# One-hots that read their iota from a PSUM bank of VectorE's own, in a two-layer graph network on one Trainium2 core

## Chip, cores and metric

One core of one Trainium2 chip runs the whole kernel as one program. The metric is the device time in microseconds from start to end of one execution. Before the change it is 2472.18 us, the median of three runs (2470.21, 2472.18 and 2474.44).

## The reference

`x` has 6250 rows (nodes) of 256 numbers, and there are 100,000 edges `src -> dst`, sorted by `dst`. Low numbers of `dst` are far more frequent than high ones. What is computed, cut to what matters:

```
xn  = layernorm(x)
agg = segment_sum(xn[src], dst);  cnt = segment_sum(1, dst)
h   = relu(agg / max(cnt,1) @ W1l.T + b1 + xn @ W1r.T)          # layer 1
agg = segment_sum(h[src], dst)
gnn = agg / max(cnt,1) @ W2l.T + b2 + h @ W2r.T                 # layer 2
mix = linear attention over all rows, layer norm, a two-layer MLP with gelu, layer norm
x   = x + gnn + mix
x   = x + ffn(layernorm(x))     # gelu(x@W1+b1), softmax over 8 experts, rows to the best expert's matrix
```

## The kernel before

The rows are cut into 49 tiles of 128, the edges into 197 superchunks of 4 x 128, taken from the highest `dst` to the lowest. For each superchunk GpSimd (POOL) issues four indirect DMAs (L686), which gather 128 rows each from DRAM into one of eight slots of a ring in SBUF. Before it refills a slot, POOL waits at L683 until TensorE has added what lay there. SyncE relays each landed superchunk to TensorE at L596.

VectorE makes the one-hots of a superchunk in one instruction at L856: 4 x 128 columns, `(dst - first row of the tile) == iota`, half precision. Two of its operands are tensors in SBUF (`dst` and `iota16`), and a third, the tile's first row in `tv`, is one number per partition. TensorE multiplies one-hots and gathered rows into the bank `AGG` (L1455), and in layer 1 also one-hots and ones into `CNT` (L1453). A pair of superchunk and tile is an item. There are 245 items in each layer. A table of words tells every engine which items end a tile. The engines take the words apart with register instructions (`Walk`, L447 to L479, whose `kept` is L460, and `Chunks` for TensorE, L481 to L507).

Layer 1 has two stages. In stage A each of 49 turns does the first part of the mixer for one tile and three items. In stage B each of 49 turns does the rest of the mixer for one tile and two items. VectorE's program of a turn of stage B is one list: two statistics, the attention's division (L973 to L978), the sum with the row (L984), nine small steps of a reciprocal root (L422 to L432), the two normalisations (L1007 and L1010), the next two one-hots (L856) and the mixer's residual (L1014). `m_t` in SBUF carries L978 to L984 and L1010 to L1014.

Wherever an item ends a tile, each engine runs its part of `finish1` between its other work. TensorE transposes the hidden rows of two tiles ago (`tr2`, L1461 into the upper half of bank `FT`), makes the product of one tile ago (`out1`, L1480 to L1485 into the lower half of `FO`), the second product of two tiles ago (`r2`, L526 into the lower half of `B7`) and transposes the mean of this tile (`tr1`, into the lower half of `FT`). `r2` waits until VectorE has added the tile before (`residual`, L899). VectorE runs `mean_of` (L883 to L874), `residual` and `hidden` (L892 and L894). ScalarE copies the transposes (L1268 and L1272), applies relu (L1259) and stores the hidden rows for layer 2.

Layer 2 has five items a turn and `finish2` at every tile's end, with much more TensorE work for the expert network. A tail sorts the rows to their experts and runs the expert matrices.

The order within an engine is the written one. Semaphores order the engines: `line.done` counts, `line.wait(e, name, t, n)` waits for that event of tile t - n.

Of the kernel before, what the change touches and what calls it, by code (L numbers as in the profile page):

```python
# [23 lines left out]
P = 128  # L24
N, C, EDGES = 6250, 256, 100000
CH = C // P
TILES = -(-N // P)
LAST_ROWS = N - (TILES - 1) * P
SC = 4
# [138 lines left out]
def build(nc, x, srcL, dstL, dst_tail, w, out):  # L168
    with ExitStack() as ctx:
# [32 lines left out]
        iota16 = sb("iota16", [P, P], F16)  # L202
# [126 lines left out]
        FH = FT[:, C:2 * C]  # L329
        FR = B7  # L330

# [115 lines left out]
        class Walk:  # L447
# [3 lines left out]
            def __init__(self, e, body, n, nu, first):  # L451
                self.e, self.nu, self.u = e, nu, 0
                self.w = e.value_load(words[0:1, n, bass.ds(body, 1)])
                self.k = body * nu + first
                self.t, self.last = self.kept(self.w % 64, TILES - 1), None
                self.c = self.chunk()
# [6 lines left out]
            def chunk(self):  # L463
                return self.kept((self.t + (SUPER - 1 - self.u) - self.k) % 256, SUPER - 1)
# [4 lines left out]
            def ends(self):  # L469

                t = self.t
                self.last = self.kept((self.w >> (6 + self.u)) % 2, 1)
                self.u += 1
                self.t = self.kept(t + self.last, TILES - 1)
                if self.u < self.nu and self.c is not None:
                    self.c = self.chunk()
                return t, self.last
# [8 lines left out]
        class Chunks(Walk):  # L486
# [3 lines left out]
            def __init__(self, e, body, n, nu, first, layer):  # L490
                self.e, self.nu, self.ready, self.items, self.u = e, nu, 1 + layer * SUPER, 1 + layer * ITEMS, 0
                self.w = e.value_load(words[0:1, 3 + n, bass.ds(body, 1)])
                self.k = body * nu + first
                self.set_counts(self.w % 256 + self.ready)
# [4 lines left out]
            def ends(self):  # L499

                k, c, self.u = self.k + self.u, self.c, self.u + 1
                stays = self.kept((self.w >> (7 + self.u)) % 2, 1)
                if self.u < self.nu:
                    self.set_counts(c + stays)
                return lambda: within(self.e, (k + self.ready - c) & 63, TILES - 1), stays
# [213 lines left out]
        def _(e):  # L719
# [13 lines left out]
            step(e.tensor_copy(iota16[:], ii[:, 0:P]))  # L733
            step(e.tensor_copy(iof[:, 0:P + 3], ii[:]))
            step(e.tensor_scalar(ident[:], iof[:, 0:P], iof[:, P + 2:P + 3], None, ALU.is_equal))
            step(e.tensor_scalar(upper[:], iof[:, 0:P], iof[:, P + 2:P + 3], None, ALU.is_gt))
            step(e.memset(ones16[:], 1.0))
# [114 lines left out]
            def one_hot(walk, layer):  # L852

                k, t, c = walk.here()
                e.wait_ge(s_sum, k + (layer * ITEMS + NS + 1 - walk.nu))
                VI.done(e.scalar_tensor_tensor(  # L856
                    S[:, walk.u, :, :], dst[:, bass.ds(c * SC, SC)].unsqueeze(2).to_broadcast([P, SC, P]),
                    tv[:, bass.ds(k, 1)], iota16[:].unsqueeze(1).to_broadcast([P, SC, P]),
                    ALU.subtract, ALU.is_equal), "S")
# [19 lines left out]
            def finish1(t, g, mix_done):  # L879
# [20 lines left out]
                if isinstance(t, int):  # L900
                    part(e, t, 0, mean_of)
                    part(e, t, 3, residual)
                    part(e, t, 2, hidden)
                else:
                    t = Turn(e, t, (0, 1))
                    mean_of(t)
                    with e.If(t.base > 2):
                        residual(t - 3)
                        hidden(t - 2)
                    with e.If(t.base == 2):  # L910
                        hidden(t - 2)
# [48 lines left out]
            def to_stats(i, first, second, items):  # L960
# [10 lines left out]
                if first:  # L971
# [7 lines left out]
                    m_t.rearrange("p (h q m) -> p h q m", h=CH, m=HD), blocks[:, :, 0:P].rearrange("p h (q m) -> p h q m", m=HD),  # L979
# [4 lines left out]
                step("s", at(lambda: e.scalar_tensor_tensor(m_s[:], xnS, rstd[:, bass.ds(raw(i), 1)], m_t[:], ALU.mult, ALU.add)))  # L984
# [14 lines left out]
            def from_stats(i, first, second, meanwhile=lambda: None):  # L999
# [10 lines left out]
                step("n2", mo(lambda: e.scalar_tensor_tensor(m_t[:], m_o, lnt[:, 2:3], lng2, ALU.subtract, ALU.mult)))  # L1010
# [3 lines left out]
                step("res", mo(lambda: e.scalar_tensor_tensor(res_tile(i - 2), m_t[:], lnt[:, 7:8], res_tile(i - 2),  # L1014
# [24 lines left out]
            def finish2(t, g):  # L1039
# [5 lines left out]
                def x2(t):  # L1045
                    PO2.wait(e, "o", t)
                    VX2.done(e.tensor_tensor(res_tile(t), res_tile(t), FO[:, 0:C], ALU.add), "x2")
# [160 lines left out]
        def _(e):  # L1208
# [46 lines left out]
            def finish1(t):  # L1255
                def relu(t):
                    PH1.wait(e, "h", t)
                    VB1.wait(e, "hlo", t, 1)
                    AR1.done(e.activation(hb[:], FO[:, 0:C], ACT.Relu), "relu")  # L1259
# [164 lines left out]
        def _(e):  # L1424
# [39 lines left out]
            def finish1(t):  # L1464
# [3 lines left out]
                def tr2(t):  # L1468
# [4 lines left out]
                    PB1.done(transposes(FT, C, hb), "tr2")  # L1473

                def out1(t):
# [3 lines left out]
                    for h in range(CH):  # L1479
                        e.matmul(FO[:, 0:C], xTs[:, h, :], w1r[:, h, :], start=(h == 0), stop=False)  # L1480
                    e.matmul(FO[:, 0:C], ones3[:], gb1, start=False, stop=False)
                    if isinstance(t, int):
                        AM1.wait(e, "mT", t)
                    for h in range(CH):
                        ins = e.matmul(FO[:, 0:C], mT[:, h, :], w1l[:, h, :], start=False, stop=(h == CH - 1))  # L1485
                    PH1.done(ins, "h")

                def r2(t):
                    AH1.wait(e, "hT", t)
                    VR1.wait(e, "res", t, 1)  # L1490
# [3 lines left out]
                def tr1(t):  # L1494
                    VM1.wait(e, "mean", t)
                    clear(AGG[:])
                    clear(CNT[:, 0:1])
                    PT1.done(transposes(FT, 0, mean), "tr1")
# [86 lines left out]
            def finish2(t):  # L1585
                def out2(t):
                    AM2.wait(e, "mT", t)
                    PO2.done(matmuls(e, FO[:, 0:C], [(mT[:, h, :], w2l[:, h, :]) for h in range(CH)]), "o")
# [30 lines left out]
                def tr1(t):  # L1619
                    VM2.wait(e, "mean", t)  # L1620
                    clear(AGG[:])
                    PT2.done(transposes(FT, 0, mean), "tr1")
# [114 lines left out]
```

## Time and profile before

| | us |
|---|---|
| median of the three runs | 2472.18 |
| lowest and highest run | 2470.21, 2474.44 |
| span of the profiled execution | 2464.9 |
| median less that span | 7.3 |
| busy: TensorE (PE), GpSimd (POOL), VectorE (DVE), ScalarE (ACT) | 1925.4, 1692.3, 1145.2, 561.3 |
| mean granted clock of TensorE, of full speed | 0.888 |

The profiled execution's own time is not listed apart from its span. The span goes from the first to the last instruction, and what lies around it is taken as the 7.3 us to the median. The profile has views of one execution: how busy each engine is, which instruction waited for which, the chain of work that ended last, groups of instructions by line, and the instructions in order of time. "Issue" is time in which an engine waited for nothing that the profile shows. A letter q behind an engine (DVEq) marks its sequencer, which runs waits and register instructions. Times in the views are counted from the start of the span.

### The profile page before, as it was taken

What the parts mean: (1) busy time and instruction counts of PE and PEld (TensorE: products, weight loads), DVE (VectorE), ACT (ScalarE), POOL (GpSimd) and SP (SyncE); (2) the same over time, 40 slices, a digit from 0 to 9 for tenths busy, and PEclk for the clock granted to TensorE, in tenths of its full rate; (3) what the DMA queues carried; (4) which work ended last, traced back from release to release, by engine and by line L of the source; (5) the groups of instructions that cost most, each with busy time, mean ns of one, the idle gap of its engine ahead of it and who ended that gap; (6) DMA issues with size and microseconds to landing.
All of it is one profiled execution on the core that took longest, in us unless ns stands there. A gap on an engine that the chain in (4) does not pass through costs nothing.

```text
span 2464.9 us, 41722 instructions
## 1 busy us (share of the span) xinstructions
PE 1925.4 (78%) x9589; PEld 1194.8 (48%) x9590; DVE 1145.2 (46%) x3187; ACT 561.3 (23%) x1270; POOL 1692.3 (69%) x1759
## 2 busy tenths in 40 slices
PE   2599988888688877786899999877764543679998
PEld 1255555555355555553455555443332211368886
DVE  6444444434377777775655555443322221252221
ACT  5544433333122222221222222111110000101110
POOL 4577777777777777775777777777777777264442
PEclk9999999989799999987999999887876665789999
DMA  5444444444444444443455545454444333235551
GB/s 175 136 125 121 126 124 121 120 119 122 121 137 132 131 134 134 134 128 106 154 174 158 172 148 174 137 164 125 151 126 132 115 115 105 97 138 167 166 167 64
DMA packets 155421, 332.58 MB, mean 135 GB/s; under 512 B 35285, under 2 KB 89527, under 8 KB 155349
## 3 DMA queue, kind: packets, MB, share of 16 engines
q0 software_dynamic: 85824, 248.21, 34.4%
q10 hardware_dynamic: 42630, 58.35, 6.8%
q1 hardware_dynamic: 26898, 25.33, 3.3%
q14 instruction: 54, 0.44, 0.1%
q8 instruction: 15, 0.25, 0.0%
HBM read 273.97 MB, written 58.72 MB: 135 GB/s over the span
## 4 chain that ended last, share of the span: by engine, by line
POOL 34%; PE 28%; issue 16%; DVE 11%; DMA 3%; DVEq 3%; POOLq 2%; ACT 2%; SPq 0%; ACTq 0%
POOL big L686 34%; PE bank L526 8%; PE bank L1687 8%; PE bank L1455 4%; PE bank L1675 2%; DVE S L856 1%; DMA mbuf<-qT_d 1%; PE bank L1461 1%; DVE m_s L984 1%; POOLq L683 1%; PE bank L1610 1%; DVE m_t L978 1%; POOL big L696 1%; DVE res L1014 1%; PE bank L1485 1%
## 5 line engine op out<-in xcount | busy, mean ns | idle before, releaser
L686 POOL DMA_INDIRECT big<-xh_d,edges x782 | 772.9, 988 | 243.6 <-issue 231.3
L686 POOL DMA_INDIRECT big<-hh_d,edges x782 | 750.1, 959 | 256.9 <-issue 231.5
L1455 PE MATMUL bank<-big,S 128*128 x1960 | 591.1, 427 | 249.0 <-SPq L596 237.1
L856 DVE SCALAR_TENSOR_TENSOR S<-edges,tv,iota 128x512 f16<-128x512 f16 x490 | 365.2, 753 | 430.0 <-PE bank L1455 289.9
L1455 PEld LDWEIGHTS bank<-big,S 128*128 128x128 f16 x1960 | 204.1, 104 | 535.8 <-issue 393.0
L1453 PE MATMUL bank<-ones,S 128*128 128x1 f16 x980 | 166.8, 170 | 72.3 <-SPq L596 55.4
L526 PE MATMUL bank<-turned,x1T 128*128 128x512 f32 x392 | 194.4, 618 | 0.0
L707 POOL DMA_INDIRECT out_dram<-big,node_s x56 | 56.8, 1014 | 145.1 <-DVE big L1189 139.0
L1383 ACT ACTIVATE x1T<-bank 128x256 f32<-128x256 f32 x49 | 18.9, 385 | 527.9 <-PE bank L1461 527.8
L1453 PEld LDWEIGHTS bank<-ones,S 128*128 128x128 f16 x980 | 96.0, 98 | 86.9 <-SPq L596 67.3
L1189 DVE SCALAR_TENSOR_TENSOR big<-bank,prob_s,res 128x256 f32<-128x256 f32 x56 | 27.1, 484 | 179.3 <-PE bank L1689 179.3
L526 PEld LDWEIGHTS bank<-turned,abuf 128*128 128x128 f32 x784 | 96.2, 194 | 24.0 <-issue 23.0
L1397 ACT ACTIVATE mbuf<-bank 128x512 f32<-128x512 f32 x98 | 58.5, 597 | 201.9 <-PE bank L526 201.9
L1687 PE MATMUL bank<-big,abuf 128*128 x448 | 101.9, 381 | 0.0
L1687 PE MATMUL bank<-big,mbuf 128*128 x448 | 101.4, 379 | 0.0
L526 PEld LDWEIGHTS bank<-turned,x1T 128*128 128x128 f32 x392 | 66.4, 189 | 69.5 <-issue 69.5
L526 PE MATMUL bank<-turned,mbuf 128*128 128x512 f32 x196 | 97.0, 619 | 0.0
L872 DVE TENSOR_SCALAR lo<-bank,RC 128x256 f32<-128x256 f32 x98 | 47.4, 484 | 103.6 <-PE bank L1455 82.0
L526 PE MATMUL bank<-turned,abuf 128*128 128x8 f32 x784 | 91.7, 252 | 0.8 <-ACT abuf L1389 0.8
L1552 PE MATMUL bank<-mbuf 128*128 128x132 f32 x196 | 35.9, 307 | 68.6 <-DMA mbuf<-qT_d 68.6
L1687 PEld LDWEIGHTS bank<-big,abuf 128*128 128x128 f32 x448 | 83.5, 191 | 10.3
L1687 PEld LDWEIGHTS bank<-big,mbuf 128*128 128x128 f32 x448 | 82.9, 190 | 10.2
(228 smaller groups left out, 2927.0 us busy)
## 6 DMA issues: line engine op xcount, KB each, us to landing
hx_d<-mbuf ACTq DMA_DIRECT2D x49, 512.0 KB
big<-xh_d,edges POOLq DMA_INDIRECT x782
big<-hh_d,edges POOLq DMA_INDIRECT x782
big<-in_fwd_dram SPq DMA_DIRECT2D x8, 1024.0 KB, 6.1
xh_d<-big SPq DMA_DIRECT2D x49, 128.0 KB, 2.2
qT_d<-abuf ACTq DMA_DIRECT2D x49, 128.0 KB
hh_d<-HL ACTq DMA_DIRECT2D x49, 128.0 KB
mbuf<-qT_d ACTq DMA_DIRECT2D x49, 128.0 KB
```

The source lines that it names most:

```text
L526: ins = eng.matmul(out_ap, a, b, start=(n == 0), stop=(n == len(pairs) - 1))
L686: e.indirect_dma_start(G[:, r, n % SC, :], None, table, bass.IndirectOffsetOnAxis(ap=srcx[:, n:n + 1], axis=0)).then_inc(d_g[r], 16)
L707: e.indirect_dma_start(out, bass.IndirectOffsetOnAxis(ap=node_s[:, i:i + 1], axis=0), o_sb[:, u, :], None, bounds_check=N - 1, oob_is_err= ...
L856: VI.done(e.scalar_tensor_tensor(S[:, walk.u, :, :], dst[:, bass.ds(c * SC, SC)].unsqueeze(2).to_broadcast([P, SC, P]), tv[:, bass.ds(k, 1 ...
L872: line.done(e.tensor_scalar(lo[:], AGG[:, C:2 * C], rc, None, ALU.mult), "lo")
L1189: VO.done(e.scalar_tensor_tensor(o_sb[:, u % OB_SLOTS, :], (B6, FT)[u % 2][:, 0:C], prob_s[:, bass.ds(i, 1)], RB[:, u, HID:HROW], ALU.mult ...
L1397: AG2.done(e.activation(Hb[:, b * 512:b * 512 + 512], pb[4 + b][:], ACT.Gelu), f"g{b}")
L1453: e.matmul(CNT[:, 0:1], S[:, walk.u, j, :], ones16[:, 0:1], start=False, stop=False, skip_group_check=True)
L1455: ins = e.matmul(AGG[:], S[:, walk.u, j, :], G[:, bass.ds(slot, 1), j, :].rearrange("p a c -> p (a c)"), start=False, stop=False, skip_gro ...
L1552: ins = e.matmul(B4[:, h * (P + 4):(h + 1) * (P + 4)], qS[:, h, :], KVs[:, h, :], start=True, stop=True)
L1675: ins = e.transpose(((B4, B5), (FO, B7))[u % 2][b][:, q * P:(q + 1) * P], RB[:, u, (b * 4 + q) * P:(b * 4 + q + 1) * P], ident[:])
L1687: e.matmul(acc, (HT, HT2)[u % 2][:, j, :], wd[:, bass.ds(ex, 1), j, :].rearrange("p a c -> p (a c)"), start=(j == 0), stop=False)
```

## The change

The constant 0 to 127 moves from `iota16` (SBUF, half precision) to `numbers_p`, the lower half of bank `FO` (PSUM, full precision), and L856 reads it there. The mixer's temporary `m_t` of stage B moves to `m_p`, the upper half of `FO`. Only VectorE uses this bank then, until the tail. To free it, the product of `out1` and `out2` goes to the upper half of `FT` (`FU`), and the transposes of `tr2` go to the upper half of `B7` (`FH`). TensorE's waits follow the banks: `tr2` now waits for `residual` of the tile before (it was `r2`), `tr1` in layer 1 waits for relu of the tile before, and `tr1` in layer 2 for `x2` of the tile before. VectorE's `finish1` does `residual` before `mean_of`. All remainders by a power of two in the walks become bit masks.

```diff
-        iota16 = sb("iota16", [P, P], F16)
...
-        FH = FT[:, C:2 * C]
+        FH = B7[:, C:2 * C]
         FR = B7
+        FU = FT[:, C:2 * C]
+        numbers_p, m_p = FO[:, 0:P], FO[:, C:2 * C]
...
-                self.t, self.last = self.kept(self.w % 64, TILES - 1), None
+                self.t, self.last = self.kept(self.w & 63, TILES - 1), None
...
-                return self.kept((self.t + (SUPER - 1 - self.u) - self.k) % 256, SUPER - 1)
+                return self.kept((self.t + (SUPER - 1 - self.u) - self.k) & 255, SUPER - 1)
...
-                self.last = self.kept((self.w >> (6 + self.u)) % 2, 1)
+                self.last = self.kept((self.w >> (6 + self.u)) & 1, 1)
...
-                self.set_counts(self.w % 256 + self.ready)
+                self.set_counts((self.w & 255) + self.ready)
...
-                stays = self.kept((self.w >> (7 + self.u)) % 2, 1)
+                stays = self.kept((self.w >> (7 + self.u)) & 1, 1)
...
-            step(e.tensor_copy(iota16[:], ii[:, 0:P]))
...
+            step(e.tensor_copy(numbers_p, iof[:, 0:P]))
...
-                    tv[:, bass.ds(k, 1)], iota16[:].unsqueeze(1).to_broadcast([P, SC, P]),
+                    tv[:, bass.ds(k, 1)], numbers_p.unsqueeze(1).to_broadcast([P, SC, P]),
...
                     t = Turn(e, t, (0, 1))
-                    mean_of(t)
                     with e.If(t.base > 2):
                         residual(t - 3)
-                        hidden(t - 2)
-                    with e.If(t.base == 2):
+                    mean_of(t)
+                    with e.If(t.base > 1):
                         hidden(t - 2)
...
-                    m_t.rearrange("p (h q m) -> p h q m", h=CH, m=HD), ...
+                    m_p.rearrange("p (h q m) -> p h q m", h=CH, m=HD), ...
...
-  step("s", ... m_s[:], xnS, rstd[:, bass.ds(raw(i), 1)], m_t[:], ...)
+  step("s", ... m_s[:], xnS, rstd[:, bass.ds(raw(i), 1)], m_p, ...)
...
-  step("n2", ... m_t[:], m_o, lnt[:, 2:3], lng2, ...)
+  step("n2", ... m_p, m_o, lnt[:, 2:3], lng2, ...)
...
-  step("res", ... res_tile(i - 2), m_t[:], lnt[:, 7:8], res_tile(i - 2), ...)
+  step("res", ... res_tile(i - 2), m_p, lnt[:, 7:8], res_tile(i - 2), ...)
...
-                    VX2.done(e.tensor_tensor(res_tile(t), res_tile(t), FO[:, 0:C], ALU.add), "x2")
+                    VX2.done(e.tensor_tensor(res_tile(t), res_tile(t), FU, ALU.add), "x2")
...
-                    AR1.done(e.activation(hb[:], FO[:, 0:C], ACT.Relu), "relu")
+                    AR1.done(e.activation(hb[:], FU, ACT.Relu), "relu")
...
-                    PB1.done(transposes(FT, C, hb), "tr2")
+                    VR1.wait(e, "res", t, 1)
+                    PB1.done(transposes(B7, C, hb), "tr2")
...
                 def r2(t):
                     AH1.wait(e, "hT", t)
-                    VR1.wait(e, "res", t, 1)
...
+                    AR1.wait(e, "relu", t, 1)
                     PT1.done(transposes(FT, 0, mean), "tr1")
...
-                    PO2.done(matmuls(e, FO[:, 0:C], [...]), "o")
+                    PO2.done(matmuls(e, FU, [...]), "o")
...
+                    VX2.wait(e, "x2", t, 1)
                     PT2.done(transposes(FT, 0, mean), "tr1")
```

In `out1` the four matmuls and the bias write `FU` in place of `FO[:, 0:C]` as well.

## Rows read from the trace of the kernel before

**Rows 1.** Timeline (start us, us) of POOL: its one wait for a slot over 0.3 us.
```profile
1377.19 1.45 POOL L686 DMA_INDIRECT big<-hh_d,edges  x1 [1.00 <-PE bank L1455]
```

**Rows 2.** Line L686: ns min/median/max, first and last start.
```profile
L686 POOL DMA_INDIRECT big<-xh_d,edges x782: 942/946/1440, 95.1 to 1104.9; - x196
```

**Rows 3.** Gathers by stretch (A, B, layer 2 to 1500, after): busy us, mean ns.
```profile
L686 POOL DMA_INDIRECT big<-xh_d,edges x428 | 424.7, 992 | 135.7 <-issue 128.3 <-DMA xh_d<-big 5.6 <-PE bank L1455 1.8
...
L686 POOL DMA_INDIRECT big<-xh_d,edges x354 | 348.2, 983 | 107.9 <-issue 103.0 <-PE bank L1455 4.9
...
L686 POOL DMA_INDIRECT big<-hh_d,edges x295 | 285.2, 967 | 108.5 <-issue 84.7 <-DMA hh_d<-HL 18.3 <-PE bank L1455 5.6
...
L686 POOL DMA_INDIRECT big<-hh_d,edges x487 | 464.9, 955 | 148.3 <-issue 146.8 <-PE bank L1455 1.5
```

**Rows 4.** Waits of PE: 300 to 650 us, then 1125 to 2113 us.
```profile
PE bank L1453 <- SPq L596: 46.4, 17, 3.8
...
PE bank L1455 <- SPq L596: 233.9, 80, 13.9
```

**Rows 5.** Timeline (start us, us): first and last gather held by a one-hot.
```profile
116.65 1.44 DVE L856 SCALAR_TENSOR_TENSOR S<-edges,tv,iota 128x512 f16<-128x512 f16 x2 [1.50 <-issue]
...
117.03 1.19 POOL L686 DMA_INDIRECT big<-xh_d,edges  x1 [0.30 <-issue]
...
1988.22 0.96 POOL L686 DMA_INDIRECT big<-hh_d,edges  x1 [0.30 <-issue]
```

**Rows 6.** Timeline: first and last gather that starts inside a PSUM-reading DVE operation.
```profile
114.14 0.48 DVE L872 TENSOR_SCALAR lo<-bank,RC 128x256 f32<-128x256 f32 x1
114.53 0.95 POOL L686 DMA_INDIRECT big<-xh_d,edges  x1 [0.31 <-issue]
...
1976.99 0.95 POOL L686 DMA_INDIRECT big<-hh_d,edges  x1 [0.30 <-issue]
```

**Rows 7.** Chain that ended last, one turn of stage B: shares, then start us, us.
```profile
by line: issue 21.2%; DVE S L856 6.5%; DVE m_s L984 5.8%; DVE res L1014 5.6%; DVEq L460 5.4%; DVE m_t L978 5.1%; DVE lnt L986 5.1%; DVEq L1028 5.1%; DVE lnt L965 4.0%; DVEq L453 3.5%; DVEq L856 3.0%; DVE lnt L423 2.9%; DVE lnt L431 2.8%; DV
...
856.41 0.31 DVEq L460
...
857.02 0.33 DVE S L856
```

**Rows 8.** Waits of DVE, 720 to 1105 us; then the next turn's one-hots in the timeline.
```profile
DVE S L856 <- issue: 7.7, 30, 0.3
...
865.66 1.55 DVE L856 SCALAR_TENSOR_TENSOR S<-edges,tv,iota 128x512 f16<-128x512 f16 x2 [0.27 <-issue]
```

**Rows 9.** Register instructions of PE's sequencer: ns min/median/max.
```profile
L497 PEldq FUSED_REGOPS  x147: 126/180/188, 97.3 to 2091.8; - x147
...
L1521 PEldq FUSED_REGOPS  x147: 82/90/135, 111.1 to 2116.1; - x147
```

**Rows 10.** DVE operations of 256 columns by form: busy us, mean ns.
```profile
L872 DVE TENSOR_SCALAR lo<-bank,RC 128x256 f32<-128x256 f32 x98 | 47.4, 484 | 103.6 <-PE bank L1455 82.0 <-issue 19.8
L874 DVE SCALAR_TENSOR_TENSOR mean<-bank,RC,lo 128x256 f32<-128x256 f32 x98 | 47.4, 484 | 3.5
...
L984 DVE SCALAR_TENSOR_TENSOR m_s<-mbuf,rstd,m_t 128x256 f32<-128x256 f32 x49 | 23.7, 484 | 11.6 <-DVE m_t L978 11.2 <-issue 0.2
...
L1051 DVE TENSOR_SCALAR m_t<-res,lnt 128x256 f32 x48 | 21.8, 453 | 1.8
...
L894 DVE TENSOR_TENSOR HL<-hb,HL 128x256 f16<-128x256 f32 x49 | 21.1, 431 | 1.7
...
L899 DVE TENSOR_TENSOR res<-res,bank 128x256 f32 x46 | 19.0, 412 | 0.0
```

**Rows 11.** Timeline, a stage-B turn that ends a tile.
```profile
889.35 1.10 PE L526 MATMUL bank<-w2r,hT 128*128 128x256 f32 x4 [1.35 <-DVE res L899]
...
894.88 0.39 ACT L1342 ACTIVATE mbuf<-bank 128x256 f32<-128x256 f32 x1 [2.07 <-PE bank L1574]
...
895.85 0.42 DVE L965 BATCH_NORM_STATS2 lnt<-mbuf 128x6 f32<-128x256 f32 x1
```

More of the change, by code:

```diff
@@ L900, in finish1 @@
                 if isinstance(t, int):
+                    part(e, t, 3, residual)
                     part(e, t, 0, mean_of)
-                    part(e, t, 3, residual)
                     part(e, t, 2, hidden)
@@ L978, in to_stats @@
                 step("tz", at(lambda: e.tensor_tensor(
-                    m_t.rearrange("p (h q m) -> p h q m", h=CH, m=HD), blocks[:, :, 0:P].rearrange("p h (q m) -> p h q m", m=HD),
+                    m_p.rearrange("p (h q m) -> p h q m", h=CH, m=HD), blocks[:, :, 0:P].rearrange("p h (q m) -> p h q m", m=HD),
                     zd.rearrange("p (h q) -> p h q", h=CH).unsqueeze(3).to_broadcast([P, CH, P // HD, HD]), ALU.mult)))
@@ L983, in to_stats @@
                     e.wait_ge(d_lx, raw(i) * 16 + 16)
-                step("s", at(lambda: e.scalar_tensor_tensor(m_s[:], xnS, rstd[:, bass.ds(raw(i), 1)], m_t[:], ALU.mult, ALU.add)))
+                step("s", at(lambda: e.scalar_tensor_tensor(m_s[:], xnS, rstd[:, bass.ds(raw(i), 1)], m_p, ALU.mult, ALU.add)))
                 after("s")
@@ L1009, in from_stats @@
                     after("n1")
-                step("n2", mo(lambda: e.scalar_tensor_tensor(m_t[:], m_o, lnt[:, 2:3], lng2, ALU.subtract, ALU.mult)))
+                step("n2", mo(lambda: e.scalar_tensor_tensor(m_p, m_o, lnt[:, 2:3], lng2, ALU.subtract, ALU.mult)))
                 got = meanwhile()
                 after("n2")
-                step("res", mo(lambda: e.scalar_tensor_tensor(res_tile(i - 2), m_t[:], lnt[:, 7:8], res_tile(i - 2),
+                step("res", mo(lambda: e.scalar_tensor_tensor(res_tile(i - 2), m_p, lnt[:, 7:8], res_tile(i - 2),
                                                               ALU.mult, ALU.add)))
@@ L1479, in out1 @@
                     for h in range(CH):
-                        e.matmul(FO[:, 0:C], xTs[:, h, :], w1r[:, h, :], start=(h == 0), stop=False)
-                    e.matmul(FO[:, 0:C], ones3[:], gb1, start=False, stop=False)
+                        e.matmul(FU, xTs[:, h, :], w1r[:, h, :], start=(h == 0), stop=False)
+                    e.matmul(FU, ones3[:], gb1, start=False, stop=False)
                     if isinstance(t, int):
@@ L1484, in out1 @@
                     for h in range(CH):
-                        ins = e.matmul(FO[:, 0:C], mT[:, h, :], w1l[:, h, :], start=False, stop=(h == CH - 1))
+                        ins = e.matmul(FU, mT[:, h, :], w1l[:, h, :], start=False, stop=(h == CH - 1))
                     PH1.done(ins, "h")
@@ L1587, in out2 @@
                     AM2.wait(e, "mT", t)
-                    PO2.done(matmuls(e, FO[:, 0:C], [(mT[:, h, :], w2l[:, h, :]) for h in range(CH)]), "o")
+                    PO2.done(matmuls(e, FU, [(mT[:, h, :], w2l[:, h, :]) for h in range(CH)]), "o")
                 def trx(t):
```

## The prediction

> **What bounds the kernel now.** I read the waits of POOL first, then the gathers by line and stretch, then PE's waits, then the chain of waits inside one turn of stage B. POOL hardly ever waits for a free slot of the ring. In layer 1 what stands before the gathers of stage B is 107.9 us for 354 of them, 0.305 us each and nearly all "issue" [rows 3]. In layer 2 it idles longer for a slot only once, 1.00 us at 1377 us [rows 1]. So both layers run at POOL's pace of 0.946 us [rows 2] plus 0.305 us a gather, and what a gather takes beyond 0.946 us is the only slack in it. That excess is 428 x 46 ns = 19.7 us in stage A, 354 x 37 ns = 13.1 us in stage B, 295 x 21 ns = 6.2 us in layer 2 up to 1500 us and 487 x 9 ns = 4.4 us after it [rows 3], some 43 us in all.
>
> The timeline shows what it is. A gather that starts while a one-hot runs lasts until shortly after the one-hot's end: at 116.65 us two one-hots run back to back (1.44 us), and the gather of 117.03 us takes 1.19 us [rows 5]. From the first to the last [rows 5] I count 131 such gathers with together 31.9 us of excess: 67 with 15.8 us in stage A, 30 with 7.8 us in stage B, 34 with 8.4 us in layer 2 (5.5 us of it after 1377 us). In stage B 18 more lie behind L984, with 1.0 us. Behind VectorE operations that read PSUM it isn't so. 125 gathers start inside L872, L874, L899, L978 or L1047, and all but one take 0.95 us or less, as the first and the last [rows 6]. (The one takes 1.05 us, and an operation with two SBUF tensors follows there.) So a one-hot with its iota in PSUM should hold no gather up.
>
> POOL isn't the only limit. In stage A TensorE waits for landed data, 46.4 us of the 350 us from 300 on [rows 4], so that POOL sets the end of stage A. In stage B the chain of a turn holds VectorE and its sequencer alone [rows 7]: it is VectorE's list that takes the time, 8.6 us a turn (its one-hots start at 857.02 us [rows 7] and at 865.66 us [rows 8]), while POOL runs ahead and is caught up only at the end. In layer 2 TensorE is close to full until about 1460 us, as the one wait for a slot shows [rows 1], and after it waits for data (233.9 us over the layer) [rows 4].
>
> **The change, part by part.**
>
> *One-hots off the gathers.* 31.9 us of excess go, where POOL's pace is what counts: 15.8 us in stage A in full. In stage B POOL gains 7.8 + 1.0 us (L984 now reads one tensor from SBUF, L1010 still reads two). In layer 2 the 2.9 us before 1377 us are lost to TensorE, and 5.5 us after it are kept. The gathers slide against the other operations, so each term may be off by a fifth.
>
> *Masks for remainders.* In stage B they are on the path. Before the first one-hot of a turn the sequencer loads a word and runs L460 with two remainders, 0.31 us [rows 7], and VectorE idles for it, 7.7 us in 30 times, 0.26 us each [rows 8]. What a remainder costs: on TensorE's sequencer L497 (one remainder, one sum) takes 180 ns, and L1521 (a sum, a difference, one mask) 90 ns [rows 9]. With one simple step less on the dearer side I take 0.12 to 0.13 us for each. Two of them are the 0.26 us. The two one-hots of a turn take 1.55 us together [rows 8], with the sequencer's remainders between them, where two back to back take 1.44 us [rows 5], so 0.11 us more go. That is 0.37 us a turn, 17.4 us over 47 full turns. If a mask costs as much as a remainder it is nothing. On POOL nothing changes, on ScalarE and TensorE the sequencers run ahead, and I count nothing.
>
> *PSUM in VectorE's own list.* Six operations of a turn read or write `FO` now (two L856, L978, L984, L1010, L1014). L874 reads one PSUM tensor and L984 none, and both take 484 ns [rows 10]; that is the same kind of instruction as the one-hot, so I take nothing. The ends: 484 less 453 ns (L872 against L1051) is 31 ns more, 412 less 431 ns (L899 against L894) 19 ns less [rows 10], so over 6 x 47 operations +8.7 or -5.4 us. Writes to PSUM by VectorE have no row, and I give them the same ends. The Trainium skill speaks against the change here (VectorE: DVE Perf Modes, the errata section): it gives a fixed 120 cycles to an operation from PSUM and 58 to one from SBUF, 65 ns more. The rows of L874 and L984 don't show it. By that rule four reads a turn would cost 12 us.
>
> *The moved wait on TensorE.* In stage B VectorE reaches `finish1` after L986. In 6 of the 11 tile ends from 687 us on, TensorE is there first, and `r2` already stands 1.35 us or less for L899 [rows 11]. Now `tr2` stands, and behind it `out1` (2.1 us, which ran meanwhile before). With `residual` first, VectorE releases it at 887.8 us, and in the same order as before TensorE is done about 1.15 us later. Behind it are the MLP's products, ScalarE's L1342 and VectorE's L965. L1342 ended at 895.27 and L965 started at 895.85 [rows 11], which would now be 895.5. So some 0.9 us a time are exposed, 5.4 us in all. In stage A the same wait costs TensorE about 0.4 us at about half of the ends, hidden by the ring, whose slots are free over 20 us before POOL needs them. `tr1` waits for relu behind `r2` (1.3 us against 0.38 us), and in layer 2 for `x2` behind 7 us of expert products: nothing. If these covers went, each would cost the length of the wait itself, under 0.5 us at 49 ends.
>
> *Setup, tail, queues.* The constant is one VectorE copy as before, no DMA is added or moved, and POOL and SyncE get no new wait: nothing.
>
> **The sum.** Stage B's list ends 15.8 + 17.4 - 5.4 = 27.8 us earlier, POOL's last gather of layer 1 15.8 + 8.8 = 24.6 us, with about 1 us of margin behind it. The later of the two decides: 25 us. Layer 2 adds 5.5 us. Together 30.5 us from a span of 2464.9 us, 2434.4 us. The median lies 7.3 us above this span, so I forecast 2441.7 us.
>
> **The rivals.**
> 1. *Masks are no cheaper than remainders.* For it: the register instructions on VectorE differ in length for other reasons too (L460 covers several steps). Against it: rows 9. Stage B gains nothing of its own, and the exposed waits shrink to about 3 us: 15.8 - 3 + 5.5 = 18 us, 2454 us. Chance 0.12.
> 2. *PSUM costs more in the list,* by the size that the skill's page gives (65 ns) on four reads a turn, 12 us: 27.8 - 12 + 5.5 = 21 us, 2451 us. The same mechanism at 31 ns on six is 8.7 us and 2448 us. Against it: 484 and 484 ns. Chance 0.13.
> 3. *The gathers are not released,* because `dst` and the scalar `tv` are still read from SBUF. Then POOL keeps its pace, VectorE's faster list only waits for data, and the gain is the 1 us of margin: 2471 us. Against it: L874 too reads a tensor and a scalar from SBUF, and no gather waits behind it. Chance 0.04.
> 4. *Slower: stage B's list itself.* Place: the six PSUM operations a turn, above all the writes of L978 and L1010, which nothing in the trace shows, and what waits on them. All other gains together are 27.8 + 5.5 = 33 us, so it decides from 33 / 282 = 118 ns an operation on. At 150 ns it is 42 us of cost, 9 us slower, 2481 us. Against it: every PSUM reader in the trace. Chance 0.04.
>
> **How the numbers follow.** The forecast has 0.67. Its own bounds are the fifth on the gathers' terms (5 us), the PSUM ends (-5 to +9 us, the gain capped by POOL's pace) and the exposed waits (0 to 5 us): 2432 to 2450 us. To hold 8 in 10 it reaches to the middle of rivals 1 and 2, to 2458 us, and on the fast side to 2431 us. Under 0.2% (5 us) a measurement of this kernel can't tell from no change. Faster by more: 0.67 + 0.12 + 0.13 = 0.92. Rival 3 is within: 0.04. Rival 4: 0.04.
>
> **What would show it.** Right: mean gathers near 0.95 us in all stretches, and those inside one-hots at 0.95 us; L460 at 0.1 to 0.2 us; turns of stage B near 8.25 us without a tile's end; one-hots still at 0.75 us; a wait of L1461 on L899 of about 2 us at 6 ends. Wrong: gathers inside one-hots still long (rival 3), L460 at 0.3 us (rival 1), one-hots or L978, L984, L1010, L1014 longer by 50 ns or later behind each other (rivals 2, 4), or many more waits of POOL for a slot, which would say that another engine took over the bound.

## Result, and the profile after

The changed kernel takes 2488.61 us, the median of four runs (2485.78 to 2497.58), against 2471.95 us for the kernel before beside it. The ratio is 1.0076, 95% interval 1.0054 to 1.0097: 0.76% slower, where the prediction said 2441.7 us and gave slower a chance of 0.04. In the new code every line below 900 lies two further down, later ones mostly one (L686 is L688, L856 is L858, L899 is L901). The page of the changed kernel:

```profile
span 2484.0 us, 45558 instructions
...
PE 1928.5 (78%) x9589; PEld 1185.4 (48%) x9590; DVE 1144.4 (46%) x3187; ACT 560.4 (23%) x1270; POOL 1655.8 (67%) x1759
...
q14 instruction: 275, 2.25, 0.3%
```

POOL is busy 36.5 us less than before (1692.3), VectorE and TensorE are busy as long as before to within 3.1 us, and the span has grown by 19.1 us. It isn't TensorE's clock, whose granted share is 0.896 after and 0.888 before. Two counts don't fit a change of banks: the instructions went from 41722 to 45558, and the DMA queue that brings code (packets, MB, share) has 275 packets, where the page of before has:

```profile
q14 instruction: 54, 0.44, 0.1%
```

The groups of the changed kernel by line answer to [rows 3] and [rows 10]:

```profile
L688 POOL DMA_INDIRECT big<-xh_d,edges x782 | 744.3, 952 | 267.0 <-issue 229.6 <-PE bank L1456 31.7 <-DMA xh_d<-big 5.6
L688 POOL DMA_INDIRECT big<-hh_d,edges x782 | 742.1, 949 | 287.1 <-issue 228.1 <-PE bank L1456 31.5 <-DMA hh_d<-HL 27.5
...
L858 DVE SCALAR_TENSOR_TENSOR S<-edges,tv,bank 128x512 f16<-128x512 f32 x490 | 365.5, 747 | 571.0 <-issue 298.1 <-PE bank L1456 268.5 <-DVE mbuf L1008 1.9
...
L1011 DVE SCALAR_TENSOR_TENSOR bank<-mbuf,lnt,turned 128x256 f32<-128x256 f32 x49 | 23.8, 485 | 0.3 <-DVEq L126 0.3
L985 DVE SCALAR_TENSOR_TENSOR m_s<-mbuf,rstd,bank 128x256 f32<-128x256 f32 x49 | 23.5, 481 | 11.3 <-DVE bank L979 11.2
...
L979 DVE TENSOR_TENSOR bank<-bank,mbuf 128x256 f32<-128x256 f32 x49 | 21.2, 433 | 1.7
```

The gathers are released: 952 and 949 ns on average, where the stretches of layer 1 had 992 and 983. Of those that start while a one-hot runs, 318 now, none takes over 0.96 us and the mean is 945 ns; before it was 230 with a mean of 1085 ns. The one-hot takes 747 ns (753 before). What is new stands in the idle time: POOL waits 63 us for slots of the ring, and the one-hots stand 298 us on "issue".

Where the 19 us are, I read from first and last starts. Stage B goes from the first to the last start of the sum with the row, layer 2 from the first to the last gather of `hh_d`. For the changed kernel (ns min/median/max, first to last start):

```profile
L985 DVE SCALAR_TENSOR_TENSOR m_s<-mbuf,rstd,bank x49: 479/481/482, 654.6 to 1113.0; 128x256 f32<-128x256 f32 x49
```
```profile
L688 POOL DMA_INDIRECT big<-hh_d,edges x782: 940/946/1719, 1128.1 to 2128.8; - x196
```

and for the kernel before:

```profile
L984 DVE SCALAR_TENSOR_TENSOR m_s<-mbuf,rstd,m_t x49: 483/484/486, 672.5 to 1109.4; 128x256 f32<-128x256 f32 x49
```
```profile
L686 POOL DMA_INDIRECT big<-hh_d,edges x782: 942/946/1717, 1124.3 to 2112.0; - x196
```

Stage B now begins 17.9 us earlier, takes 458.4 us instead of 436.9 (21.5 more), layer 2 takes 1000.7 instead of 987.7 (13.0 more), and what follows the last gather 355.2 instead of 352.9. So stage A brought what was hoped for, and stage B and layer 2 each lost something of their own. The same rows of every later kernel give the table further down.

In stage B, it is mostly the tile ends: the nine turns with one took 11.1 to 12.8 us before and take 11.1 to 15.2 us now, 16.7 us more in all. The 39 others are 0.12 us longer each, 4.8 us in all. The waits from 654 to 1113 us (us in total, times, longest):

```profile
PE bank L1462 <- DVE res L901: 21.4, 9, 3.3
```

This is the moved wait. The timeline of one such turn (start us, us) shows what stands behind it:

```profile
928.71 0.43 DVE L987 BATCH_NORM_STATS2 lnt<-m_s 128x6 f32<-128x256 f32 x1
929.37 0.42 DVE L901 TENSOR_TENSOR res<-res,bank 128x256 f32 x1 [0.23 <-issue]
...
929.93 0.66 PE L1462 MATMUL bank<-ident,hb 128*128 128x128 f32 x2 [3.27 <-DVE res L901]
...
930.39 1.91 PE L1482 MATMUL bank<-w,xTs 128*128 128x256 f32 x4
...
932.55 1.45 PE L1487 MATMUL bank<-w,mT 128*128 128x256 f32 x4
...
933.84 1.03 PE L528 MATMUL bank<-w2r,hT 128*128 128x256 f32 x4
...
935.51 1.06 PE L528 MATMUL bank<-x1T,turned 128*128 128x128 f32 x8
...
937.79 0.75 DVE L858 SCALAR_TENSOR_TENSOR S<-edges,tv,bank 128x512 f16<-128x512 f32 x1 [1.32 <-PE bank L1456]
```

TensorE idles 3.27 us, then does `out1` (until 934 us), which before ran while `r2` was not yet due, then `r2`, the new mean's transpose and the mixer's products, and only then the item whose sum VectorE's second one-hot waits for.

For layer 2 the waits of VectorE from 1205 to 2113 us, after and before:

```profile
DVE S L858 <- issue: 224.6, 150, 7.9
DVE S L858 <- PE bank L1456: 188.8, 75, 7.9
```
```profile
DVE S L856 <- PE bank L1455: 233.2, 99, 5.2
...
DVE S L856 <- issue: 69.1, 124, 1.8
```

The one-hots wait 155 us longer for nothing that the profile names, up to 7.9 us at once, while 239 of the 275 code packets arrive in this stretch (19 before). Much of this takes the place of other waits, such as the one-hots' own on TensorE (44 us less); layer 2 as a whole is 13.0 us longer.

### The profile page after: what moved, and what is told of

Read it like the earlier page. It is cut to its first block, busy times and chain, and to the rows that moved or that the text cites. A ratio compares the mean times of both kernels' runs of the same rounds, so it can differ in the third digit from the quotient of the medians.

```text
span 2484.0 us, 45558 instructions
## 1 busy us (share of the span) xinstructions
PE 1928.5 (78%) x9589; PEld 1185.4 (48%) x9590; DVE 1144.4 (46%) x3187; ACT 560.4 (23%) x1270; POOL 1655.8 (67%) x1759
## 3 DMA queue, kind: packets, MB, share of 16 engines
q14 instruction: 275, 2.25, 0.3%
## 4 chain that ended last, share of the span: by engine, by line
PE 36%; POOL 20%; issue 17%; DVE 13%; DVEq 6%; DMA 3%; ACT 3%; POOLq 1%; ACTq 1%; SPq 0%
POOL big L688 19%; PE bank L528 11%; PE bank L1690 8%; PE bank L1456 6%; PE bank L1678 2%; DVEq L462 2%; PE bank L1462 2%; PE bank L1487 2%; PE bank L1482 1%; DMA mbuf<-qT_d 1%; DVE m_s L985 1%; PE bank L1612 1%; DVE bank L979 1%; DVEq L455 1%; DVEq L858 1%
## 5 line engine op out<-in xcount | busy, mean ns | idle before, releaser
L688 POOL DMA_INDIRECT big<-hh_d,edges x782 | 742.1, 949 | 287.1 <-issue 228.1
L688 POOL DMA_INDIRECT big<-xh_d,edges x782 | 744.3, 952 | 267.0 <-issue 229.6
L858 DVE SCALAR_TENSOR_TENSOR S<-edges,tv,bank 128x512 f16<-128x512 f32 x490 | 365.5, 747 | 571.0 <-issue 298.1
```

The source lines that it names most:

```text
L688: e.indirect_dma_start(G[:, r, n % SC, :], None, table, bass.IndirectOffsetOnAxis(ap=srcx[:, n:n + 1], axis=0)).then_inc(d_g[r], 16)
L858: VI.done(e.scalar_tensor_tensor(S[:, walk.u, :, :], dst[:, bass.ds(c * SC, SC)].unsqueeze(2).to_broadcast([P, SC, P]), tv[:, bass.ds(k, 1 ...
```

## Experiments

A remainder of an unbounded register can be negative, and a wait on it must not be. So kernels with remainders have one mask more on each loaded word, the "guard":

```diff
-                self.w = e.value_load(words[0:1, n, bass.ds(body, 1)])
+                self.w = e.value_load(words[0:1, n, bass.ds(body, 1)]) & ((1 << 24) - 1)
```

The first four kernels asked for the parts of the change.

**e2, masks alone:** the kernel before with the five `%` as `&`.

> The kernel before, with the five remainders written as masks and nothing else changed; before's median is 2472. Theory: the masks are not fused as the remainders were, so the loops' code is longer: stage B's turns take 0.1 us more in some 36 of them (4 us), layer 2's loop is fetched again in each turn (instruction queue from 54 packets to about 275) and costs 10 to 15 us, the tail 2: 2486 to 2493 us, with the gathers' mean as before. Rival A (layer 2 lost its time to the moved banks): instruction queue higher perhaps, but the time within 5 us of 2476. Rival B, the prediction as it was written: 0.37 us less per turn of stage B, 2454 us.

**e1, remainders:** the changed kernel with the five `&` as `%` and the guard.

> The changed kernel with the five masks back as remainders (each loaded word gets one mask, since a remainder of an unbounded word can be negative); the changed kernel's median is 2489. Theory: stage A keeps its gain of 18 us, layer 2 gains about 5 by the shorter gathers instead of losing 13, the instruction queue goes back to about 54 packets, and the long tile ends of stage B stay (13 to 15 us in about nine turns): 2464 to 2472 us. Rival A (layer 2's loss is the first transpose's wait on the second residual sum): 2482 to 2487 us with the queue at 54 packets. Rival B (no effect of masks at all): 2489.

**e3, banks alone:** e1 with

```diff
-        numbers_p, m_p = FO[:, 0:P], FO[:, C:2 * C]
+        numbers_p, m_p = iota16[:], m_t[:]
```

> As the changed kernel with remainders, but with the iota and the second mean's scratch back in SBUF: only the moved banks, their waits and VectorE's new order are left of the change. Theory (iota in PSUM is worth 18 us in stage A, up to 9 in the rest of layer 1 and 5 in layer 2; the moved waits cost about 20 in stage B): the gathers' mean back at 967 to 992 ns and 2485 to 2497 us, 20 to 30 above the same kernel with both in PSUM. Rival (the gathers are not what sets stage A, and the banks cost nothing): 2470 to 2476.

**e4, the product first:** e1 with

```diff
                     with e.If(t.base > 1):
-                        tr2(t - 2)
                         out1(t - 1)
+                        tr2(t - 2)
                         r2(t - 2)
```

and the wait for `mT` moved from `tr2` into `out1`, which also waits for relu of the tile before now (`tr2` keeps its own wait for relu).

> As the changed kernel with remainders, but in a tile end TensorE issues the first layer's product ahead of the transposes that now wait for VectorE's residual sum. Theory: the wait of those transposes (20 us in 8) is covered by the product and falls under 8 us, the long tile ends go from 13 to 15 us back to about 12, and the time is 8 to 20 us below the same kernel without this edit: 2448 to 2460. Rival A (the tile ends are long because VectorE has more to do between two one-hots, whatever TensorE's order is): within 3 us of the kernel without this edit. Rival B: the product now waits for ScalarE's transposed mean where the transposes used to run, and it is 3 to 8 us slower.

Four more ran as controls and to find whose code is fetched again. **e0** is the kernel before with the guard, **e5** the changed kernel with remainders (and guard) in `Chunks` alone, which only TensorE uses, **e6** the changed kernel with the product first, **e7** both of these together (expected: 2448 to 2453 us).

> The kernel before with one mask added to each loaded word, as the kernels with remainders here have it: the control for them. Theory: some 340 more register operations of 40 ns, most of them beside other work: 2472 to 2476 us, stage B between 437 and 441 us long, the stretch after the last gather between 353 and 358. Rival (the added mask is nothing, and stage B's 442 us in the kernel with the product first are the cost of the new banks and of VectorE's order): stage B at 437 and 2472 us.

> The changed kernel (2489) with remainders on TensorE's queue alone; VectorE and ScalarE keep the masks. Masks alone on the kernel before left the instruction queue at 55 packets, both together have 275. Theory (TensorE's loop of layer 2 is the code that is fetched again): 54 packets, layer 2's gathers end after 980 to 986 us instead of 1001, layer 1 keeps the 3 us that VectorE's masks win: 2465 to 2471 us. Rival (VectorE's code is what is fetched again, since it grew most): 275 packets still, and 2486 to 2490 us.

> The changed kernel as it is, masks everywhere, with TensorE's product ahead of the transposes. Theory: the 18 us of the tile ends come back and nothing else: 2467 to 2473 us, instruction queue still about 275 packets and layer 2 at 1001 us. Rival (what is fetched again hangs on where the loop lies and not on its length, so moving three waits can end it): about 55 packets, layer 2 at 983 and 2450 to 2455 us.

They fell on a chip on which the kernel before takes 3107.0 us (3095.71 to 3130.37). Their times can't be set beside the others, but the number of code packets of a kernel is the same on both kinds of chips (e6: 275 on each, e0: 54 on each). e5, e6 and e7 have 275: with TensorE's code short again, the fetches stay, so it isn't TensorE's code. The rival of e5 was right. It is VectorE's or ScalarE's, and the idle one-hots say VectorE's. The loop of layer 2 stands twice in VectorE's program alone. The first copy is run three times, the second 45 times from 1198.8 us on:

```profile
L1090 DVEq FUSED_REGOPS  x45: 80/80/80, 1198.8 to 2087.2; - x45
```

Both kernels have three code packets between 1203 and 1219 us, in the first pass of that copy. Before has none after them until 1303 us. The changed kernel has the next at 1219.8 us, just after the second pass began (1218.1 us), and then several in each pass.

A listing of VectorE's instructions in order puts that copy at 1071 to 1365 in the changed kernel and at 1108 to 1402 in e2, equally long. The listing is of the built program and not of a trace, and its numbers are not addresses; what counts is the distance of 37. Hence:

**e8, 37 instructions more:** the changed kernel with

```diff
+        pad = sb("pad", [1, 37])
...
+            for n in range(37):
+                e.memset(pad[:, n:n + 1], 0.0)
             one_hots(0, 2, ITEMS_2, 0, 1)
             with e.Fori(0, SPLIT_AT) as i:
                 turn2(i)
```

> The changed kernel (2489) with 37 one-element memsets of VectorE ahead of layer 2's loops, and nothing else. The extra fetches begin in turn 3 of layer 2, where VectorE goes over to the second copy of its loop. In the kernel before with masks (55 packets) that copy is as long as here, 294 instructions, and lies 37 instructions later. Theory (where VectorE's loop lies against the 8 kB pieces in which code is fetched decides whether it stays): with the 37 instructions in front the queue falls from 275 packets to about 55, layer 2's gathers end after 981 to 987 us and not 1001, and the kernel with more instructions is faster: 2470 to 2476 us. Rival (length, or TensorE's loop, decides): 275 packets, 2489 to 2492 us.

**e6b** is e6 again, **e9** has the product first and the 37 memsets, **e0b** is e0 again.

> The same kernel as in the run of the product first with masks everywhere, on another chip. Theory: the 18 us of stage B's tile ends come back against the changed kernel, the queue stays at 275 packets and layer 2 at 1001 us: 2468 to 2474 us. Rival: 2450 to 2455 us, if the long tile ends were where the refetched code cost its time.

> The changed kernel with the product first and the 37 memsets: both losses taken away, masks everywhere. Theory: 2489 less 18 for the tile ends less 16 for the fetches: 2452 to 2458 us, about what remainders with the product first gave (2455). Rival (masks win 5 us in layer 1, as stage B of the kernel before with masks had it): 2447 to 2451 us.

> The kernel before with one mask added to each loaded word, on another chip than the first time. Theory: stage B 437 to 441 us, the stretch after the last gather 353 to 358 us, 2472 to 2476 us in all. Rival (the guard is what made the kernels with remainders slower in stage B by 5 us): stage B at 442 us and 2477 us.

All of them, with before and after from above, by the rows named (each stage's time, in us, is from the profile of one execution). The kernel before had 2472.01 us beside e1 to e4 and 2470.86 us beside e8 to e0b.

| kernel | median | ratio to before [95%] | B begins | stage B | layer 2 | rest | code packets |
|---|---|---|---|---|---|---|---|
| before | 2471.95 | 1 | 672.5 | 436.9 | 987.7 | 352.9 | 54 |
| after | 2488.61 | 1.0076 [1.0054, 1.0097] | 654.6 | 458.4 | 1000.7 | 355.2 | 275 |
| e2 masks alone | 2470.3 | 0.9997 [0.9985, 1.0008] | 667.3 | 431.9 | 990.6 | 357.5 | 55 |
| e0b guard alone | 2476.17 | 1.0018 [1.0007, 1.0030] | 672.5 | 442.9 | 989.2 | 356.3 | 54 |
| e3 banks alone | 2497.03 | 1.0096 [1.0079, 1.0113] | 675.3 | 458.5 | 989.2 | 358.1 | 54 |
| e1 remainders | 2471.44 | 1.0001 [0.9991, 1.0011] | 656.0 | 460.5 | 982.3 | 358.1 | 54 |
| e4 product first | 2455.18 | 0.9934 [0.9917, 0.9950] | 654.3 | 442.0 | 985.6 | 356.2 | 54 |
| e8 memsets | 2475.7 | 1.0018 [1.0007, 1.0029] | 655.8 | 460.0 | 985.4 | 357.6 | 55 |
| e6b product first, masks | 2472.93 | 1.0016 [1.0000, 1.0033] | 653.8 | 442.9 | 999.8 | 357.6 | 275 |
| e9 both | 2459.1 | 0.9957 [0.9941, 0.9974] | 653.9 | 443.8 | 984.9 | 353.1 | 55 |

What follows:

- *The moved wait.* e1 to e4 takes 18.5 us from stage B and 16 us from the time, after to e6b 15.5 and 16. In e4 the waits from 654 to 1096 us are

```profile
PE bank L1462 <- DVE res L901: 0.4, 1, 0.4
```

  and the tile-end turns are back at 11.0 to 12.6 us. From the other side, e0b to e3 adds the banks, their waits and VectorE's order alone: 15.6 us in stage B and nothing in layer 2. Rival A and B of e4 are out.
- *The iota in PSUM.* e3 to e1 moves only the iota and `m_t`: the time falls by 25.6 us, stage B begins 19.3 us earlier, layer 2 is 6.9 us shorter, and stage B itself 2.0 us longer. e3's gathers are held again, those of stage A that start inside a one-hot by 20.3 us in all (beyond 0.946 us each):

```profile
L689 POOL DMA_INDIRECT big<-xh_d,edges x782 | 779.3, 997 | 258.0 <-issue 230.0 <-PE bank L1457 22.4 <-DMA xh_d<-big 5.6
```

- *Code fetched again.* 37 instructions of VectorE that do nothing make the changed kernel 13 us faster, so it is VectorE's code that was fetched again. Layer 2 is 15.3 us shorter (14.9 from e6b to e9), and the idle one-hots are gone, in e8 from 1205 to 2113 us:

```profile
q14 instruction: 55, 0.45, 0.1%
```
```profile
DVE S L859 <- PE bank L1459: 216.3, 92, 4.8
...
DVE S L859 <- issue: 89.8, 133, 1.9
```

  My expectation for e2 (2486 to 2493 us, 275 packets) was wrong for the same reason: the masks lengthen the loop from 270 to 294 listed instructions in e2 too, but there it lies well.
- *Masks.* They gain 5.0 us in stage B of the kernel before and 5.2 ahead of it, lose 4.2 between stage B and layer 2 (POOL's last gather of layer 1 starts at 1101.0 us, when VectorE's list is through at 1099.2), 2.9 in layer 2 and 4.6 after it, and e2's time is that of before. The guard costs 5 us, 6.0 of it in stage B, so e1 and e4 carry a handicap that the changed kernel doesn't have.
- *Expectations.* e8, e6b, e1 and e4 came out within the ranges of their theories. e3 came 0.03 us above its own and e9 1 us. Of e0b the rival was right: the guard isn't hidden beside other work.
- *Best version:* e4, 0.66% under before on this chip. Leaving out its guard might bring up to 5 us more, which wasn't tried, since nothing would bound the waits then. e9 has no guard and isn't faster.

Still open was why masks gain 5 us in stage B of e2 and nothing in the new order of banks (e9 443.8 us, e4 442.0 with a guard worth 6). e10 and e11 are e6 with 37 and 64 memsets ahead of stage B's loop, and e12 is e0, e13 is e4 with 37 there.

> The product first, masks everywhere, and the 37 memsets ahead of stage B's loop rather than of layer 2's: VectorE's stage-B loop then begins at instruction 641 (637 in the kernel before with masks, 604 without the memsets); layer 2's loops lie as in the run that had 55 packets. Theory (stage B too hangs on where its loop lies): stage B 432 to 438 us instead of 443 to 444, the second one-hot 770 to 800 ns after the first instead of 894, 2446 to 2454 us. Rival (position does nothing there, masks and banks interact otherwise): stage B at 442 to 445, 2455 to 2460 us.

> The same with 64 memsets: stage B's loop at instruction 668, layer 2's second copy at 1135 to 1429. Theory: another position, another stage B, somewhere from 432 to 448 us, and by the three-piece picture of layer 2 (a loop of 294 instructions stays unless it reaches into a fourth 8 kB piece) still about 55 packets. Rival: stage B at 442 to 445 as without memsets.

> The kernel before with the guard mask (stage B 443 us, 2476 us) and 37 memsets ahead of stage B's loop, which moves it from instruction 602 to 639, and layer 2's second copy (272 long) from 1032 to 1069. Theory: stage B changes by more than 3 us, probably to 436 to 440; and if the second copy now reaches into a fourth piece, some 275 packets and 10 to 18 us more in layer 2, so 2470 or 2486 us. Rival (position does nothing where there is no refetch): stage B at 442 to 444 and 2474 to 2478 us.

> The product first with remainders (2455 us) and 37 memsets ahead of stage B's loop, which moves it from instruction 569 to 606. Theory (position counts in stage B): stage B moves from 442 by more than 3 us, either way, the rest as it was: 2448 to 2462. Rival (it does not): 442 plus or minus 1 and 2455 to 2458 us, the memsets' own 2 us included.

These four, and e10 and e13 once more (e10b and e13b, with the same expectations), fell on two chips, where the kernel before takes 3108 us (e10 to e13, the chip of e0 and e5 to e7) and 3059 us (e10b and e13b). Their times, which scatter by 0.5 to 1.7% from run to run, can't show a few us. But in the turns without a tile's end the median gaps between the starts of VectorE's operations are nearly the same on all chips, and they answer the question. In ns:

| kernel | stage B's loop | from L993 to L422 | from the first one-hot to the second |
|---|---|---|---|
| e2 (masks, old banks) | 637 | 769 | 775 |
| after, e8, e6b, e9; e5, e6, e7 | 604 | 869 | 901 |
| e10, e10b (moved by 37) | 641 | 769, 768 | 775 |
| e11 (moved by 64) | 668 | 744 | 775 |
| before (remainders) | not listed | 872 | 801 |
| e0, e12 (guard; moved by 37) | 602, 639 | 889, 1041 | 801, 801 |
| e4, e13 (guard, product first; moved by 37) | 569, 606 | 878, 888 | 801, 801 |

(L993 and L422 of the kernel before: the second statistic's end and the first small step of the reciprocal root.) From e6 to e10 nothing but the place of the loop changes, and the two gaps fall by 100 and 126 ns to those of e2. Between the one-hots all of it lies in one spot, ahead of one register instruction, which starts 506 ns after the first one-hot in e6 and 377 ns after it in e10. So the theory of e10 held for the gaps: where the loop lies was worth 0.23 us a turn, some 9 us in 39 turns as an estimate, of the 11.9 us between e2 and e9. It can go the other way too, as e12 shows with 152 ns more. Whether e10 takes some 2450 us on a chip like the first (2459.1 of e9 less 9, an estimate) was not measured.

The packets say something as well: e10 and e12 have 55, e13 54, and e11 66. In e11 the first copy of layer 2's loop, which is run three times, moves from 766 to 830. Between 1632 and 1694 us it has 14 packets where the same passes of e10 have 3, and VectorE goes over to the second copy only at 1703.0 us. So the picture that position decides held once more, though the expectation for e11 looked at the second copy alone. The expectation for e12 feared 275 packets and got 55.

On the two chips:

| kernel | ratio to before [95%] | code packets |
|---|---|---|
| e0, e12 (remainders, old banks) | 1.0012 [0.9979, 1.0044], 0.9983 [0.9947, 1.0020] | 54, 55 |
| e13, e13b (remainders, product first) | 1.0300 [1.0216, 1.0384], 1.0403 [1.0315, 1.0491] | 54 |
| e10, e10b, e11 (masks, product first) | 1.0564 [1.0474, 1.0653], 1.0569 [1.0472, 1.0666], 1.0559 [1.0452, 1.0665] | 55, 55, 66 |
| e5, e7, e6 (masks on VectorE) | 1.0679 [1.0606, 1.0752], 1.0674 [1.0607, 1.0741], 1.0710 [1.0643, 1.0777] | 275 |

## Why the prediction was wrong

The forecast's span was 2434.4 us and 2484.0 came, 49.6 us more. 28.6 of them arose up to the end of stage B, which was to come 25 us earlier and came 3.6 later, 18.5 in layer 2 (5.5 less forecast, 13.0 more measured), and 2.5 elsewhere. Two terms of the sum failed, the masks (17.4 us that didn't come) and the moved wait (5.4 us for 15.6 to 18.5), and a third cost, code fetched again (15 us), had no term.

1. **One-hots off the gathers: right in mechanism and size.** 15.8 us in stage A were predicted, 17.9 came in the changed kernel, and 19.3 from e3 to e1, where the held gathers had cost 20.3. In layer 2 it was 5.5 predicted, 6.9 measured. The 8.8 us of POOL's pace in stage B were worth nothing, as VectorE's list sets the time there, which the prediction said itself. They count only where that list gets shorter than POOL's, which the forecast expected and which didn't happen.
2. **Masks for remainders: wrong, 17.4 us predicted.** The step that failed is "with one simple step less on the dearer side I take 0.12 to 0.13 us for each", from [rows 9]. The term took the price of a remainder from two instructions that differ in more than the remainder, and took the mask as otherwise the same instruction. But here a remainder is one step of a fused instruction, and the mask splits it. Before, then after, at the line that bounds a value:

```profile
L460 DVEq FUSED_REGOPS  x973: 51/302/332, 92.3 to 2096.5; - x195
```
```profile
L462 DVEq ALU_OP  x1817: 40/45/57, 92.2 to 2112.3; - x182
L462 DVEq FUSED_REGOPS  x1260: 47/95/189, 92.2 to 2111.9; - x180
```

   973 instructions with a median of 302 ns became 3077, whose shorter times are eaten up by their number. In e2 the first one-hot of a turn, where the prediction saw 0.26 us to gain, starts 0.05 us later after L1010 than before (medians 770 and 716 ns), and the second follows the first after 775 ns and not 801. Alone the masks saved 5.0 us in stage B (e2), under a third of the term and mostly ahead of L422, and the whole kernel nothing. In the changed kernel, with the loop elsewhere, even that is gone (901 ns, 869 ns). Rival 1 ("masks are no cheaper") was the nearest, at a chance of 0.12.
3. **PSUM in VectorE's list: right.** Nothing was predicted between -5.4 and +8.7 us. L985 takes 481 ns (484), the write of L979 433 (425), that of L1011 485 (473), the one-hot 747 (753). 8 + 12 - 3 - 2 x 6 = 5 ns a turn. The rule of the Trainium skill (VectorE: DVE Perf Modes, the errata section), by which an operation from PSUM would take 65 ns more, is not seen in these rows. Rivals 2, 3 and 4 fall with it: 4 had the sign, but not the place.
4. **The moved wait: right mechanism, mis-sized.** 0.9 us at 6 ends were predicted, 5.4 us in all. Stage B paid 15.6 us (e0b to e3) to 18.5 us (e1 to e4), 1.7 to 2.1 us at nine. I took the ends from those where TensorE already waited in the old order. But a wait ahead of `out1` is met earlier by the length of `out1`, so that more ends meet it, and each for longer (3.27 us where 1.35 was read). And I followed what is queued behind it only to the MLP and L965, not to the item whose sum the second one-hot needs (1.32 us at 937.79 us).
5. **Not in the prediction at all: code.** Longer walks put VectorE's layer-2 loop where it is fetched anew each turn, some 15 us. The step "on ScalarE and TensorE the sequencers run ahead, and I count nothing" asked after the time of instructions, never after their room. Nor is there a term for where stage B's loop lies, 0.23 us a turn by e6 and e10.

The sum by measured terms: -17.9 in stage A; +21.5 in stage B, of which the wait is 15.6 to 18.5 and most of the rest is the 0.10 us more between the two one-hots (901 ns, 801 before) in 39 turns; +13.0 in layer 2, from +15 for the fetches, -7 for the gathers and about 5 not told apart, of which 3 go with the masks (e1 to e8, and before to e2); +2.3 in the rest. With about 0.2 between the stages that is the 19.1 us of the span. The rest of the kernel moves between 353 and 358 us from one kernel to the next without pattern, e9 with 353.1 and e6b with 357.6 having the same instructions there, 37 places apart.

## What to carry to other kernels

Releasing a gather that VectorE holds up is worth its full length only where POOL sets the pace. Check for each stage which list is the bound before adding up. When a wait is moved ahead of work in an in-order queue, price the wait by when the engine would now arrive, and follow everything queued behind it up to the engine that sets the turn; moving the ready product ahead of it gave all of it back here. After any edit to register arithmetic in a long loop, compare the instruction count and the packets of the code queue before reading anything else. A few us from such an edit may be due to where the loop has come to lie: move it by some idle instructions and measure again.

## What the runs showed of the hardware

- **Where a loop lies can cost as much as a wait.** A packet of the code queue is 8 kB (2.25 MB in 275). The changed kernel fetches 220 more than e8, in 45 turns of that copy, 4.9 a turn. The Trainium skill (Advanced Engine Details and Errata, ISA Cache) gives an engine's instruction cache as 32 KB in only two lines of 16 KB, or 256 instructions, and TensorE 128 KB. By these lines, as an estimate, a loop of 294 instructions stays loaded if it lies in two of them and not if it touches a third, and one assumption on how far the listing lags behind the real addresses (172 to 183 instructions, modulo 256) agrees with all that was seen: the second copy at 1071 refetched, those at 1108, 1135, and of 272 instructions at 1069 and 1032 not, the first copy at 830 refetched, at 766 and 803 not. TensorE's code shows no such fetches in any run. No run measured the cache's size itself, and pieces of 8 kB, of which three stay, would fit too. Neither gives the count: three lines of 16 KB a turn would be six packets, four pieces of 8 kB four, and 4.9 were fetched. The gaps of stage B that moved by 100, 126 and 152 ns have no packets beside them, and what makes them isn't known.
- **On some chips single register instructions stand for long.** On the two chips where before takes 3107 and 3059 us, many stand for 0.7 and some for 1.4 us, and the code queue has too few packets to explain it. Of VectorE's register and branch instructions 214 of 4755 take over 0.5 us in e0 and 577 of 6727 in e5, in before and after on the first chips none. TensorE's granted clock is lower there too (0.80 in e0, 0.888 before), and no run tells cause and effect apart. In e10b at the bounding line, where the same code has a longest of 57 and 189 ns elsewhere:

```profile
L463 DVEq ALU_OP  x1817: 1/45/1396, 91.6 to 2872.6; - x182
L463 DVEq FUSED_REGOPS  x1260: 1/95/1381, 91.7 to 2870.8; - x180
```

  The waits of VectorE's one-hots on "issue" are, in e0 and in e5:

```profile
DVE S L856 <- issue: 394.7, 272, 17.4
```
```profile
DVE S L858 <- issue: 808.4, 319, 21.8
```

  With the product first, the masks cost 1.6 to 2.6% more there than remainders (e10 against e13), and refetched code 1.4% more again (e6 against e10). Even the best version is 3 to 4% slower than before there, though its gathers are released as elsewhere (953 and 949 ns in e13, which is the best version with 37 memsets). Why wasn't found. A gain of 0.66% found on one chip isn't one on every chip.
